# First Horner application in four 32x32 tiles a unit, third in 64x32, and a new step order on all five engines

## What is computed

```
xn = layernorm(x)                                   # x: (4, 256, 256)
q, k, v, z = split(xn @ w_qkvz.T)                   # 32 heads of 64
q, k, v = causal depthwise conv of 4 taps;  q, k L2-normalised
for each token t, per head:                         # the recurrence
    S = S * exp(g_t);  delta = (v_t - k_t @ S) * beta_t
    S = S + outer(k_t, delta);  o_t = q_t @ S
attn = (o * rsqrt(mean(o*o)) * norm_weight * sigmoid(z)) @ w_out.T
ffn  = fwht(silu(gate(fwht(xn))) * up(fwht(xn))) @ W_down.T, with scales
out  = x + attn + ffn
```

## Time and profile before

| | |
|---|---|
| median of 3 runs | 920.72 us (919.37 to 922.29) |
| the profiled execution | 921.86 us, its span 920.0 us, mean granted clock 0.967 |
| PE busy | 845.0 us (92% of the span), 13354 instructions |
| DVE busy | 703.3 us (76%), 1248 instructions |
| ACT, POOL busy | 256.0 us (28%), 287.7 us (31%) |
| DMA | 49.56 MB, mean 54 GB/s |

### The profile page before, as it was taken

One profiled execution on the slowest core, in us unless ns is written; L12 is line 12 of the kernel. 1 busy time (PEld: TensorE's weight loads), 2 busy tenths in 40 slices (PEclk: granted clock), 3 DMA queues, 4 the chain that ended last, 5 costly groups with the idle time before them and its releaser, 6 DMA issues.

```text
span 920.0 us, 30578 instructions
## 1 busy us (share of the span) xinstructions
PE 845.0 (92%) x13354; PEld 607.2 (66%) x13354; DVE 703.3 (76%) x1248; ACT 256.0 (28%) x560; POOL 287.7 (31%) x194
## 2 busy tenths in 40 slices
PE   1887499999999999999999999999999999998685
PEld 1533267766767676767676677767777767767574
DVE  5675968888887979788887878797978888795522
ACT  2333114132332314141423223241414132331000
POOL 2019531514124242324142322423231513233110
PEclk9989699999999999999999999999999999999877
DMA  4323031131413131413213141304131231210101
GB/s 124 128 58 81 6 77 36 31 82 30 94 30 83 23 80 37 69 32 64 60 31 82 30 94 24 89 19 77 42 58 44 41 84 30 60 31 14 30 2 46
DMA packets 129157, 49.56 MB, mean 54 GB/s; under 512 B 110977, under 2 KB 120449, under 8 KB 128897
## 3 DMA queue, kind: packets, MB, share of 16 engines
q1 hardware_dynamic: 129024, 47.62, 23.8%
HBM read 39.98 MB, written 7.60 MB: 52 GB/s over the span
## 4 chain that ended last, share of the span: by engine, by line
PE 60%; DVE 17%; SPq 7%; DMA 6%; POOL 5%; issue 3%; ACT 1%; POOLq 0%; DVEq 0%; ACTq 0%
PE bank L581 17%; DVE kq L224 4%; PE bank L645 4%; PE bank L593 3%; PE bank L747 3%; SPq L512 3%; PE bank L662 3%; PE bank L749 3%; PE bank L692 3%; PE bank L602 3%; PE bank L664 3%; PE bank L730 2%; PE bank L668 2%; PE bank L719 2%; PE bank L678 2%
## 5 line engine op out<-in xcount | busy, mean ns | idle before, releaser
L581 PE MATMUL bank<-xnT,wq 128*128 128x512 f32 x512 | 261.8, 636 | 15.8 <-DVE kq L224 15.5
L224 DVE SCALAR_TENSOR_TENSOR kq<-bank,cw,kq 128x510 f32<-128x510 f32 (+2 forms) x288 | 214.6, 745 | 44.9 <-ACT kq L798 37.8
L581 PEld LDWEIGHTS bank<-xnT,wq 128*128 128x128 f32 x512 | 90.7, 195 | 98.1 <-issue 70.3
L948 POOL TENSOR_TENSOR ost<-ost,cst 128x8 f32<-128x8 f32 x32 | 52.3, 1634 | 191.7 <-DVE ost L357 191.7
L798 ACT ACTIVATE kq<-bank,cw 128x512 f32<-128x512 f32 x96 | 65.8, 685 | 143.3 <-PE bank L581 142.5
L944 POOL TENSOR_TENSOR Sd<-St,dec 128x256 f32<-128x256 f32 x32 | 19.9, 621 | 231.7 <-DVE St L345 161.4
L938 POOL TENSOR_TENSOR kqg<-kq,rows 128x1024 f32<-128x1024 f32 x32 | 75.5, 2358 | 39.0 <-DVE kq L224 39.0
L645 PE MATMUL bank<-kq 64*64 64x128 f32 x1024 | 69.0, 274 | 11.6 <-DVE kq L224 8.9
L911 POOL TENSOR_TENSOR kd<-kc,stat 128x512 f32<-128x512 f32 x32 | 33.4, 1042 | 144.1 <-DVE stat L261 144.1
L747 PE MATMUL bank<-wo,oT 128*128 128x256 f32 x256 | 70.6, 389 | 1.6 <-DVE oT L369 1.6
L270 DVE TENSOR_TENSOR ATP<-bank,gb 128x512 f32<-128x512 f32 x64 | 44.1, 689 | 30.4 <-issue 14.3
(11 more groups left out here) (132 smaller groups left out, 1449.1 us busy)
## 6 DMA issues: line engine op xcount, KB each, us to landing
rows<-decay_rows SPq DMA_DIRECT2D x64, 256.0 KB, 4.6
wq<-wqkvz_dram SPq DMA_DIRECT2D x16, 512.0 KB, 3.7
inverse_blocks<-UU SPq DMA_DIRECT2D x16, 256.0 KB, 2.0
woraw<-wout_dram SPq DMA_DIRECT2D x16, 128.0 KB, 2.2
wguT<-wgu_dram SPq DMA_DIRECT2D x8, 256.0 KB, 5.2
base_blocks<-ATP SPq DMA_DIRECT2D x128, 16.0 KB, 2.7
NT<-base_blocks SPq DMA_DIRECT2D x16, 128.0 KB, 2.1
U<-inverse_blocks SPq DMA_DIRECT2D x128, 16.0 KB, 2.0
```

Source lines behind the costliest of these rows:

```text
L224: nc.vector.scalar_tensor_tensor(out=y[:, :, t:S], in0=p[:, :, 0:S - t], scalar=cw[:, m, i // 2, 3 - t:4 - t], in1=y[:, :, t:S], op0=ALU.m ...
L581: last = nc.tensor.matmul(ring[i % 2][:], wq[:, q, kc, i // 2, :], xnT[:, kc, (i % 2) * 512:(i % 2) * 512 + 512], start=kc == 0, stop=kc = ...
L948: nc.gpsimd.tensor_tensor(ost[:, 2, :], ost[:, 1, :], k("neghalf")[:, 0:B * 2], ALU.pow).then_inc(rms_done, 1)
```

## The change

Two parts of `hz` change in shape. In the first application (j = 1) each unit's two matmuls of 64x64 weights, one a head, become four of 32x32 weights: the upper 32 rows with the upper 32 columns of `Q`, the lower with the lower, for each head; 48 columns pass as before, and the 32x32 corner is left out of this application. In the third (j = 3) the weights are the first 32 columns of `Q` alone (64 rows by 32), and the result is written to the upper partitions of each head alone; the lower ones keep what the first application left. DVE's instructions are the same.

Beside this, the strings that order the steps are new on all five engines. The starting letter of each string is shifted as well (it starts elsewhere in the cycle), so letters can't be compared between the two; relative to proj of the same pair every step still works on the pair it worked on before.

```diff
--- before.py
+++ after.py
@@ -456,10 +456,10 @@
                 dve.sem_inc(rows_made, 1)
 
                 program({"proj": proj, "ff": ff, "e": e, "stats": stats, "gram": gram, "vtr": vtr, "inv": inv, "hz": hz, "ks": ks,
-                         "state": state, "norm": norm, "gated": gated, "turn": turn, "out": out}, """K.out.0 K.turn.1 K.out.1 M.e M.stats K.out.2 K.out.3 M.gram.0 L.hz.0.0 L.hz.0.1 M.gram.1 M.vtr.0 L.hz.1.0 L.hz.1.1
-                         M.gram.2 L.hz.2.0 L.hz.2.1 M.ff M.gram.3 L.hz.3.0 L.hz.3.1 A.proj.0 L.state.0 M.vtr.1 L.ks.1 A.proj.1 M.inv.0 L.state.1
-                         A.proj.2 L.ks.2 M.inv.1 L.norm.0 L.state.2 A.proj.3 L.ks.3 L.gated.0 M.inv.2 L.turn.0 L.norm.1 A.proj.4 L.gated.1
-                         A.proj.5""")
+                         "state": state, "norm": norm, "gated": gated, "turn": turn, "out": out}, """M.hz.3.0 M.hz.3.1 A.vtr.1 P.proj.0 M.state.0 P.proj.1 M.ks.1 A.inv.0 P.proj.2 M.state.1 A.inv.1 M.ks.2 M.norm.0
+                         P.proj.3 M.state.2 M.gated.0 M.ks.3 A.inv.2 M.turn.0 P.proj.4 M.norm.1 P.proj.5 M.gated.1 M.out.0 M.turn.1 P.e P.stats
+                         M.out.1 M.out.2 P.gram.0 M.out.3 P.gram.1 A.hz.0.0 P.vtr.0 A.hz.0.1 A.hz.1.0 P.gram.2 A.hz.1.1 P.ff A.hz.2.0 A.hz.2.1
+                         P.gram.3""")
                 dve.wait_ge(acc_done, PAIRS * 4)
 
             @block.sync
@@ -561,7 +561,7 @@
                 oload(0, 0, True)
                 fload(0, 0, True)
                 sp.dma_start(yacc[:], xt).then_inc(res_in, 16)
-                program({"load": load, "rload": rload, "fload": fload, "oload": oload, "bout": bout, "bin": bin_, "uout": uout, "uin": uin}, """M.rload M.fload L.bout L.bin A.load L.uout L.uin L.oload""")
+                program({"load": load, "rload": rload, "fload": fload, "oload": oload, "bout": bout, "bin": bin_, "uout": uout, "uin": uin}, """K.bin L.rload M.load L.fload K.oload K.uout K.uin L.bout""")
 
             @block.tensor
             def _(pe):
@@ -656,16 +656,19 @@
                     n = W3
                     for i in range(HALF):
                         u = H * HALF + i
+                        if j == 1:
+                            for rs, cs in ((top, slice(0, H2)), (low, slice(H2, C))):
+                                for h in range(2):
+                                    last = nc.tensor.matmul(M[H][rs[h], i * n:i * n + n], Q[rs[h], u, cs], U16[rs[h], u, C - n:C], start=True, stop=True)
+                            continue
                         for h in range(2):
                             dst = M[H][hs[h], i * n:i * n + n]
                             if j == 0:
                                 last = nc.tensor.matmul(dst, ATP[hs[h], q, u, 0, :], T16[hs[h], u, 0:n], start=True, stop=True)
-                            elif j == 1:
-                                last = nc.tensor.matmul(dst, Q[hs[h], u, :], U16[hs[h], u, C - n:C], start=True, stop=True)
                             elif j == 2:
                                 last = nc.tensor.matmul(M[H][top[h], i * n + n - H2:i * n + n], Q[low[h], u, 0:H2], X[low[h], q, u, H2:C], start=True, stop=True)
                             else:
-                                last = nc.tensor.matmul(M[H][hs[h], i * n + n - H2:i * n + n], Q[hs[h], u, :], X[hs[h], q, u, H2:C], start=True, stop=True)
+                                last = nc.tensor.matmul(M[H][top[h], i * n + n - H2:i * n + n], Q[hs[h], u, 0:H2], X[hs[h], q, u, H2:C], start=True, stop=True)
                     last.then_inc(hz_ready, 1)
 
                 def ks(m, q, c):
@@ -776,10 +779,10 @@
                     pe.wait_ge(xh_done, m + 1)
                     nc.tensor.matmul(spare[m][:], k("had"), wdT[:, 2 * m:2 * m + 2, :], start=True, stop=True).then_inc(wd_ready, 1)
                 program({"proj": proj, "ff": ff, "ktr": ktr, "vtr": vtr, "qsq": qsq, "gram": gram, "hz": hz, "ks": ks, "delta": delta,
-                         "state": state, "o": o, "turn": turn, "out": out}, """M.proj.4 K.ks.3 M.ktr.1 K.delta.3 K.turn.0 K.o.1 M.proj.5 K.out.0 K.out.1 M.proj.6 M.vtr.0 K.turn.1 M.proj.7 K.out.2
-                         K.out.3 M.ff L.hz.0.0 L.hz.0.1 M.gram.1 L.hz.1.0 L.hz.1.1 M.gram.2 L.hz.2.0 L.hz.2.1 M.gram.3 L.hz.3.0 L.hz.3.1
-                         A.proj.0 L.delta.0 M.vtr.1 L.state.0 A.proj.1 L.ks.1 M.qsq L.delta.1 A.proj.2 L.state.1 L.o.0 L.ks.2 A.proj.3 L.delta.2
-                         A.ktr.0 L.state.2 A.gram.0""")
+                         "state": state, "o": o, "turn": turn, "out": out}, """K.hz.1.0 L.gram.2 K.hz.1.1 K.hz.2.0 L.gram.3 K.hz.2.1 L.vtr.1 K.hz.3.0 K.hz.3.1 M.proj.0 K.delta.0 M.proj.1 K.state.0
+                         L.qsq K.ks.1 M.proj.2 K.delta.1 M.proj.3 K.state.1 K.o.0 M.ktr.0 K.ks.2 M.proj.4 K.delta.2 M.ktr.1 K.state.2 M.gram.0
+                         K.ks.3 K.turn.0 K.delta.3 M.proj.5 K.o.1 K.out.0 K.out.1 M.vtr.0 M.proj.6 K.turn.1 M.proj.7 K.out.2 M.ff K.out.3
+                         M.gram.1 L.hz.0.0 L.hz.0.1""")
 
             @block.scalar
             def _(act):
@@ -883,8 +886,8 @@
                 act.wait_ge(nw_in, 32)
                 nc.scalar.activation(nwh[:], nwh[:], ACT.Copy, scale=0.5).then_inc(nwh_done, 1)
                 act.wait_ge(nwh_done, 1)
-                program({"proj": proj, "ff": ff, "dec": dec_, "ktr": ktr, "qsq": qsq, "qsum": qsum, "inv": inv, "delta": delta, "norm": norm, "oload": oload}, """A.ktr.0 L.delta.3 A.proj.4 A.ktr.1 L.norm.1 A.proj.5 M.inv.2 A.proj.6 A.proj.7 A.ff A.qsq P.proj.0 M.delta.0 P.proj.1
-                         M.oload M.delta.1 A.qsum P.proj.2 M.norm.0 M.delta.2 P.proj.3 P.dec""")
+                program({"proj": proj, "ff": ff, "dec": dec_, "ktr": ktr, "qsq": qsq, "qsum": qsum, "inv": inv, "delta": delta, "norm": norm, "oload": oload}, """K.delta.2 M.proj.4 M.ktr.1 K.delta.3 L.inv.2 M.proj.5 K.norm.1 M.proj.6 M.proj.7 M.ff A.proj.0 M.qsq L.delta.0 A.proj.1
+                         A.proj.2 M.qsum L.delta.1 M.oload A.proj.3 L.norm.0 A.dec A.ktr.0""")
 
             @block.gpsimd
             def _(pool):
@@ -955,7 +958,7 @@
                 nc.gpsimd.memset(T16[:], 0.0).then_inc(preset, 1)
                 nc.gpsimd.memset(X[:], 0.0).then_inc(preset, 1)
                 nc.gpsimd.memset(Q[:], 0.0).then_inc(preset, 1)
-                program({"root": root, "gb": gb, "kd": kd_p, "kqg": kqg_p, "sd": sd, "norm": norm}, """P.kqg.0 P.kd.0 P.gb.0 P.root P.gb.1 P.kqg.1 A.sd.1 P.kd.1 A.sd.2 A.norm.0 A.norm.1""")
+                program({"root": root, "gb": gb, "kd": kd_p, "kqg": kqg_p, "sd": sd, "norm": norm}, """A.gb.1 A.kd.0 A.kqg.0 A.kqg.1 M.sd.1 M.sd.2 A.kd.1 M.norm.0 M.norm.1 P.gb.0 P.root""")
 
 
 def finish(nc, sem, yacc, out):
```

## The result

The changed kernel takes 970.89 us (median of 4 runs, 968.84 to 977.42) against 920.79 us for the kernel before on the same chip; the ratio is 1.056 (95% interval 1.050 to 1.061). The forecast was 923.5, its range 908 to 936.

The account below looks back on a forecast made before the run. TensorE was taken as the bound, 49.8 of 50.18 us a pair its own work. Work -0.49 and waits +0.75 gave +0.26 a pair, +3.6 over 14 pairs, about 1 less at the end: 923.5 us, range 908 to 936.

Parts of the forecast that it names:

- Third application: TensorE's hz.3: 64x32 weights run at the pace of 32 columns, 1.09 us instead of 1.93, -0.84 us a pair.
- First application, its own pace: TensorE's hz.1: four 32x32 tiles side by side, 85 ns a unit, 1.36 us against 1.85, -0.49 a pair.
- rivals B and C: hz.1: B, two tiles at a time, 934 us, chance 0.19; C, four at the weights' pace with collision, 918, 0.11.
- 25 ns floor: TensorE's small matmuls: the skill's start-to-start minimum, 3.2 us for 128, left out because the trace showed 15.8 ns.
- Changes of tile size: TensorE, new order: extra visits to 32x32 (+0.40), to 64x32 (+0.10) and stretches in 128x128 (+0.34 us a pair).
- the sum's prices: TensorE's work per pair: 0.20 us a 32x32 visit, 0.17 a 128x128 stretch; in all -0.49 us a pair.
- SP's bout and NT: SP's queue: bout starts 0.85 us ahead of proj.0, NT is there 8.6 us after it; little gained or lost.
- oload: ACT's step waiting for wo: ready 12.5 us after proj.0, where ACT arrives at 10.1; no cost.
- some 4 us of issues and 2.2 us to land: SP's wo transfer: the time from bin's issue at 6.3 us to wo's landing 12.5 us after proj.0.
- no cost, with 1.9 us of cover: ACT behind oload: proj.3 done by 13.7 us, DVE wants it at 15.6 at the earliest.
- Rival E: ACT's wait for wo, 2.4 us later than reckoned, makes proj.3 late on DVE: 0.5 us a pair, 930 us, chance 0.05.
- The collision, "the price I add": DVE's inv.1 held by POOL's sd.2 and kd.1: 1.1 us, raising waits at ks.3 and turn.1 by 0.75 a pair.

Follow-up runs that it names:

- wo_first_third: The changed kernel with SP's oload issued right behind bin, ahead of rload, and old matmuls in the first application (third stays 64x32): 918.42 us.
- oload_late: The changed kernel with ACT's oload moved behind ktr.0, to the end of its iteration: 931.09 us.
- forms_only: The kernel before, old step order, with both new tile forms (four 32x32 in the first application, 64x32 in the third): 939.16 us.
- order_only: The changed kernel's new step order with the old matmuls of the kernel before in hz: 943.58 us.
- kd_late: The changed kernel with ACT's oload behind ktr.0 and also POOL's kd.1 moved behind norm.0: 1010.4 us.

## Right and wrong, step by step

The sum of a pair, from the steps' spacing on TensorE over 13 pairs: 50.18 before; third application -0.65; order by itself +0.97; four tiles -0.29 with the exits they add; stops +1.58 (small ones in hz.3 included); wait ahead of ktr.1 +1.83, proj.4 +0.09; the steps behind the wait +0.85, most of it the clock (these steps take 1.35 us more than in wo_first_third in the eight pairs with the low clock, 0.15 in the other five). That is 54.56, and 54.55 was measured.

- **Third application:** right. Halves of 0.53 and 0.60 us where 0.51 and the exit were expected.
- **First application, its own pace:** right, and rivals B and C are out. In the trace four tiles start together every 42.6 ns, so 85 ns a unit. The 25 ns floor that was left out would have made 3.2 us of 1.5.
- **Changes of tile size:** half. For the order without the four tiles the sum's prices give +0.20 and +0.34; the measured +0.97 holds some 0.1 of waits, so about 0.9. Which change costs more than its price no run takes apart.
- **SP's bout and NT:** right. bout starts 1.0 to 1.6 us ahead of proj.0 (0.85 in the forecast), and DVE begins inv.0 8.24 us after it in 10 of 13 pairs, where the forecast took 8.6.
- **oload:** this step failed, in two places. "some 4 us of issues and 2.2 us to land" took the median landing of the kernel before, where nothing stood ahead of that transfer, for one behind 1.8 MB; the issue came when reckoned (8.2 to 11.0 us after proj.0), the landing after 5.2 to 7.6 us, and oload began at 14.7 to 16.9 instead of 12.5. And "no cost, with 1.9 us of cover" asked only when DVE wants proj.3. The list of what stands behind oload (proj.3, norm.0, dec) ended one step short: ktr.0 is next, TensorE's ktr.1 needs it first, and the cover was 13.6 - 12.5 = 1.1 us.
- **Rival E** named the right mechanism, with a chance of 0.05 and 0.5 us a pair. It was about 3 us late instead of 2.4, met TensorE and not DVE, and cost 2.7 us a pair with the clock.
- **The collision, "the price I add":** the mechanism was right, the size too large. inv.1 is longer by 0.75 us (2.75 against 2.00), not 1.1, and at ks.3 the wait of 0.9 measured 0.2 to 0.3 in oload_late. It showed at the places named: ahead of ks.3, and 0.49 us ahead of turn.1 in every second pair, as forecast. In the changed kernel itself it is hidden behind ktr.1's wait.
- **Not thought of at all:** that 64 more instructions a half could run TensorE out of instructions. The profile of before gave the warning: q8's packets, the count of instructions, and 3.34 us for its shortest block against the 1.5 us I was planning. That 1.5 us is too short it doesn't show; the packets' 3.26 us from start to start and the 2.2 to 2.9 us to the end of a stop came from the runs.
- **The clock:** the sum priced waits at their length. The 1.8 us a pair at ktr.1 cost 0.8 more behind it.

Without wo's late landing and the stops the forecast would have been near: oload_late less its stops is 931.1 - 13 x 0.87 = 919.8, beside 923.5. In part that is luck, since errors cancel. TensorE's own work was forecast at -0.49 us a pair and comes to about 0 (-0.65, -0.29, some +0.9); the waits at ks.3 and turn.1 were forecast at +0.75 and come to about +0.1. The direction, slower, was given 0.47, for another reason than the ones that made it so; the range of 908 to 936 left out the case that happened.

What stays open: why an instruction packet starts when it does. That a stop falls on a boundary is shown by the moving places and by padding, and that it ends with a packet by the 2.2 to 2.9 us. That rload's traffic makes the packet start late is only argued, from the stops of 2 to 3 us beside it; and why packets start late ahead of hz.1.0, behind long blocks and with a DMA share under 0.05, nothing here shows.

## What to carry over

Before you price a moved transfer, add up the bytes issued ahead of it on the same queue, and before you call its waiter covered, go through every step queued behind the waiter up to the first that another engine needs. When a change makes more and smaller instructions, count them per microsecond: find the shortest stretch in which the kernel now uses up 256, and treat anything shorter as unproven. No two packets started less than 3.26 us apart here. And take a wait of 2 us on TensorE at more than its length, for the clock often goes with it (in 8 of 13 pairs here).

## What the hardware showed that was not expected

- TensorE's instructions come in packets of 16 KB, 256 each, no two starting less than 3.26 us apart in 14 profiles. The changed kernel's 24 stops last 0.3 to 1.7 us and end 2.2 to 2.9 us after a packet's start; beside 1 MB of rows in flight forms_only has stops of 1.9 to 3.2 us, ending 2.6 to 3.4 us after one.
- Four 32x32 tiles work side by side: four matmuls of 48 columns every 42.6 ns, 0.70 us for 64.
- The granted clock fell to 0.50 behind 8 of the changed kernel's 13 waits at ktr.1 (1.4 to 3.3 us), behind 2 of order_only's 3 of 1.45 to 1.65, and behind all 13 of kd_late's 3.5 us and more, and stayed low through 3 us and more of unbroken work. Behind order_only's waits of 0.3 to 0.9 us it did not fall. Stops for instructions of 1.9 to 3.2 us in forms_only had the same effect in 4 of 5 cases.
- DVE's two L306 beside POOL's sd.2 took 0.90 instead of 0.56 us, its two L310 beside kd.1 0.98 instead of 0.57. The Trainium skill ("SBUF — State Buffer", Who interferes with whom) has them exclude each other for a whole instruction; the trace agrees in that the instruction caught, the second L306 or the first L310, ends 0.12 us behind the end of POOL's, while the L306 that had begun 0.16 us ahead of sd.2 takes its usual 0.26.
